# Two-layer MoE stack: the second experts' weights loaded from the inputs in five transfers per tile, and the fills of the recurrence issued in sixteen paced pieces

## The reference

```python
h = _layernorm(x) * (1 + ca) + sa
x = x + ga * _L0_attn_ref(h, ...)      # RWKV-6: 2 heads of 64, a recurrence over 1024 tokens
h = _layernorm(x) * (1 + cb) + sb
x = x + gb * _L0_ffn_ref(h, ...)       # top 1 of 16 experts, 128 -> 256 -> 128, gelu
h = _layernorm(x) * (1 + ca) + sa      # from here the second layer's modulation
x = x + ga * _L1_attn_ref(h, ...)      # 16 heads of 32, second-order linear attention
h = _layernorm(x) * (1 + cb) + sb
x = x + gb * _L1_ffn_ref(h, ...)       # the second experts
```

```python
h = silu(xf @ w1) * (xf @ w3)          # w1, w3: (expert, 128, 704)
y = h @ w2                             # w2: (expert, 704, 128)
out = sum of the two chosen y, weighted
```

## Time and profile before

| | us |
|---|---|
| median of 3 runs | 745.98 (743.45 to 750.7) |
| the profiled execution | 753.16 |
| its span | 751.4 |
| TensorE matmul busy | 676.9 (90%) |
| TensorE weight load busy | 571.8 (76%) |
| VectorE, ScalarE, GpSimd busy | 424.1, 303.3, 275.9 |
| share of the span at full TensorE clock, mean | 0.926 |
| SP's queue, transfers on 16 engines | 57.21 MB, 25.0% |
| instruction queues | 1.43 and 0.25 MB, 0.8% and 0.1% |

### The profile page before, as it was taken

The page is one execution under the profiler, slowest core; times in us unless marked ns, Lnnn a source line. Parts: engine busy times, 40 slices in busy tenths (PEclk is TensorE's granted clock), DMA queues, the critical chain, the costliest instruction groups (busy, mean ns, idle before and its releaser), DMA issues.

```text
span 751.4 us, 26349 instructions
## 1 busy us (share of the span) xinstructions
PE 676.9 (90%) x10932; PEld 571.8 (76%) x10932; DVE 424.1 (56%) x1342; ACT 303.3 (40%) x1017; POOL 275.9 (37%) x419
## 2 busy tenths in 40 slices
PE   5788989989756997999999999999999799999996
PEld 4466767668746985888878787888877698898995
DVE  3776786875421323567667666566766455444443
ACT  1455565542022413545544444444443243333321
POOL 2455564556462012024252425252423242222215
PEclk9699898896765997999999999899999899999999
DMA  7999000000055410000000000000040256657562
GB/s 198 311 335 193 2 2 2 3 8 23 22 166 153 135 46 9 3 10 6 16 18 11 18 10 18 10 15 15 11 146 12 85 208 212 220 202 239 180 218 62
DMA packets 50998, 66.73 MB, mean 89 GB/s; under 512 B 5424, under 2 KB 40464, under 8 KB 47936
## 3 DMA queue, kind: packets, MB, share of 16 engines
q1 hardware_dynamic: 44992, 57.21, 25.0%
q0 software_dynamic: 3424, 7.08, 2.9%
q10 hardware_dynamic: 2464, 0.76, 0.4%
HBM read 49.44 MB, written 19.91 MB: 92 GB/s over the span
## 4 chain that ended last, share of the span: by engine, by line
PE 53%; DVE 3%; DMA 2%; issue 2%; POOL 1%; another core or an unknown queue 1%; ACT 0%; SPq 0%; DVEq 0%; POOLq 0%
PE quad L1763 6%; PE bank L1905 5%; PE bank L1788 4%; PE quad L1887 4%; PE quad L1889 4%; PE pair L1725 3%; PE bank L1812 3%; DMA f_xg<-moe_slots 2%; PE bank L1825 2%; PE quad L1769 2%; PE pair L1727 2%; PE pair L1726 2%; PE bank L1828 2%; PE bank L1815 2%; PE pair L1750 2%; PE bank L1794 2%
## 5 line engine op out<-in xcount | busy, mean ns | idle before, releaser
L2162 DVE TENSOR_TENSOR h_masked<-quad,const 128x1536 f32<-128x1536 f32 (+2 forms) x66 | 112.5, 1704 | 67.6 <-PE quad L1769 45.4
L1999 ACT ACTIVATE f_sa<-quad 128x256 f32<-128x256 f32 (+1 forms) x115 | 40.2, 352 | 94.0 <-PE quad L1889 76.7
L2276 DVE TENSOR_TENSOR f_hid<-f_sa,quad 128x256 f32<-128x256 f32 (+1 forms) x115 | 43.0, 380 | 54.1 <-ACT f_sa L1999 53.9
L1887 PE MATMUL quad<-f_xT,wall 128*128 128x256 f32 (+1 forms) x190 | 51.3, 352 | 3.7 <-DVE f_hid L2276 3.6
L1905 PE MATMUL bank<-wall,f_hid 128*128 128x128 f32 x390 | 50.7, 277 | 1.1 <-DVE f_hid L2279 0.9
L1905 PEld LDWEIGHTS bank<-wall,f_hid 128*128 128x128 f32 x390 | 47.8, 192 | 3.6 <-DVE f_hid L2279 2.8
L1889 PE MATMUL quad<-f_xT,wall 128*128 128x256 f32 (+1 forms) x190 | 50.2, 346 | 0.0
L2385 POOL DMA_INDIRECT moe_slots<-g_pay,g_slot x28 | 28.4, 1013 | 59.2 <-DVE g_pay L2130 41.2
L1976 ACT ACTIVATE h_gT<-bank 128x128 f32<-128x128 f32 x64 | 17.8, 278 | 75.0 <-PE bank L1815 75.0
L1763 PE MATMUL quad<-h_qk 32*128 32x128 f32 x1024 | 48.0, 303 | 0.0
L1788 PE MATMUL bank<-h_qk,h_state 32*32 32x128 f32 x1024 | 45.8, 276 | 1.3 <-issue 1.2
(11 more groups left out here) (410 smaller groups left out, 1888.7 us busy)
## 6 DMA issues: line engine op xcount, KB each, us to landing
wall<-moe_w SPq DMA_DIRECT2D x23, 1088.0 KB, 5.2
moe_slots<-blank SPq DMA_DIRECT2D x2, 2112.0 KB, 25.6
wall<-in_experts_dram SPq DMA_DIRECT2D x1, 4120.0 KB, 21.6
e_w<-in_experts_dram SPq DMA_DIRECT2D x15, 257.5 KB, 3.0
moe_slots<-blank SPq DMA_DIRECT2D x1, 1984.0 KB, 9.6
moe_slots<-e_yg SPq DMA_DIRECT2D x7, 256.0 KB, 2.3
f_xg<-moe_slots SPq DMA_DIRECT2D x12, 132.0 KB, 4.3
moe_w<-in_moe_w_dram SPq DMA_DIRECT2D x1, 1408.0 KB, 7.6
```

Source lines behind the costliest of these rows:

```text
L1887: pe.matmul(up_bank(n, f)[:, 0:s], w[:, F1 + TAIL1 + f * P:F1 + TAIL1 + (f + 1) * P], x_of(n)[:, 0:s], start=True, stop=True)
L1999: act.activation(sa[g % 3][:, 0:s], up_bank(n, f)[:, 0:s], ACT.Silu).then_inc(f_sa, 1)
L2162: dve.tensor_tensor(masked[k % 4][:, :, a * P:z * P], quad[:, :, a * P:z * P], cst("causal")[:, None, a * P:z * P].to_broadcast([P, HPG, ( ...
L2276: dve.tensor_tensor(hid[n % 2][:, f, 0:s], sa[g % 3][:, 0:s], up_bank(n, f)[:, T1:T1 + s], ALU.mult)\
```

## The change

It has three parts. (1) The buffer `moe1_w`, its staging copies and its semaphore `s_w2` go away. `weights(n)` loads a tile's weights straight from the inputs `moe_w3`, `moe_w1` and `moe_w2` in five transfers, which all add to the tile's semaphore (80 in place of 16). (2) The zero rows of the last block of `w2` are written by three memsets of VectorE at the start of `layer1_phase`, once for each buffer, since the fifth transfer writes only the upper 64 partitions. (3) The three remaining fills are cut into 4, 4 and 8 pieces, and SP waits before each: piece n (0 to 15) is issued when `s_tot` has reached 2n + 1.

```diff
+SPARES, WALLS = ((0, 8), (8, 16), (16, 24), (24, 31)), 4
...
+FILLS1 = 8
+SLAB1 = SLOTS1 // T1 // (FILLS1 // 2)
...
             sp.wait_ge(s_set, 3)
-            staged = t["moe1_w"].rearrange("e p n -> p e n")
-            w1, w3 = t["moe_w1"].rearrange("e p n -> p e n"), t["moe_w3"].rearrange("e p n -> p e n")
-            sp.dma_start(staged[:, :, 0:F1], w3).then_inc(s_w2, 16)
-            sp.dma_start(staged[:, :, F1:F1 + TAIL1], w1[:, :, MAIN1:F1]).then_inc(s_w2, 16)
-            sp.dma_start(staged[:, :, F1 + TAIL1:2 * F1], w1[:, :, 0:MAIN1]).then_inc(s_w2, 16)
...
-            sp.dma_start(wall[:, :, :], t["experts0"].rearrange("e p n -> p e n")).then_inc(s_wall, 16)
+            def pace(n):
+
+                sp.wait_ge(s_tot, 2 * n + 1)
+
+            spare = t["moe0_slots"][0:USED_ROWS, :].rearrange("(q p) n -> p q n", p=P)
+            for n, (a, b) in enumerate(SPARES):
+                pace(n)
+                sp.dma_start(spare[:, a:b, :], blank[:, 0:1, 0:C].to_broadcast([P, b - a, C])).then_inc(s_slab, 16)
+            for n in range(WALLS):
+                e = slice(n * E0 // WALLS, (n + 1) * E0 // WALLS)
+                pace(len(SPARES) + n)
+                sp.dma_start(wall[:, e, :], t["experts0"][e].rearrange("e p n -> p e n")).then_inc(s_wall, 16)
             slots = t["moe1_slots"].rearrange("(q k p) n -> k p q n", k=2, p=P)
-            for k in range(2):
-                sp.dma_start(slots[k], blank[:, k:k + 1, :].to_broadcast([P, SLOTS1 // T1, PAY])).then_inc(s_fill, 16)
+            for n in range(FILLS1):
+                k, q = n % 2, slice(n // 2 * SLAB1, (n // 2 + 1) * SLAB1)
+                pace(len(SPARES) + WALLS + n)
+                sp.dma_start(slots[k][:, q, :], blank[:, k:k + 1, :].to_broadcast([P, SLAB1, PAY])).then_inc(s_fill, 16)
...
-                    pe.wait_ge(f_w[n % NB], n // NB * 16 + 16)
+                    pe.wait_ge(f_w[n % NB], n // NB * 80 + 80)
...
+            for k in range(NB):
+                dve.memset(wt[k][TAIL1:P, 2 * F1 + MAIN1:], 0.0).then_inc(f_blank, 1)
...
-            sp.wait_ge(s_w2, 16 * (5 + E1_LIVE))
             sp.wait_ge(s_early, 2)
...
-                sp.dma_start(wt[n % NB][:, :], t["moe1_w"][bass.ds(e, 1), :, :].rearrange("e p n -> p (e n)"))\
-                    .then_inc(f_w[n % NB], 16)
+                w, done = wt[n % NB], f_w[n % NB]
+                w2 = t["moe_w2"][bass.ds(e, 1), :, :]
+                sp.dma_start(w[:, 0:F1], t["moe_w3"][bass.ds(e, 1), :, :].rearrange("e p n -> p (e n)")).then_inc(done, 16)
+                w1 = t["moe_w1"][bass.ds(e, 1), :, :].rearrange("e p n -> p (e n)")
+                sp.dma_start(w[:, F1:F1 + TAIL1], w1[:, MAIN1:F1]).then_inc(done, 16)
+                sp.dma_start(w[:, F1 + TAIL1:2 * F1], w1[:, 0:MAIN1]).then_inc(done, 16)
+                sp.dma_start(w[:, 2 * F1:2 * F1 + MAIN1].rearrange("p (f n) -> p f n", f=FULL1),
+                             w2[:, 0:MAIN1, :].rearrange("e (f p) n -> p (e f) n", p=P)).then_inc(done, 16)
+                sp.dma_start(w[0:TAIL1, 2 * F1 + MAIN1:], w2[:, MAIN1:F1, :].rearrange("e p n -> p (e n)"))\
+                    .then_inc(done, 16)
```

More of the change, by code:

```diff
@@ L189, in bass_adaln_stack @@
                 layer1_phase(nc, t, const, x_sb, x_bc, eps_pow, sbw[:, 1], mod_col, mod_row, quad, bank, pair, cst,
-                             hT_all, W1, s_w1, s_w2, s_fill, gate_rows, yt, weight, slot0, s_back, wall, h_all,
+                             hT_all, W1, s_w1, s_fill, gate_rows, yt, weight, slot0, s_back, wall, h_all,
                              out)
@@ L1442, in up @@
                 if n == 0:
-                    pe.wait_ge(s_wall, 16)
+                    pe.wait_ge(s_wall, 16 * WALLS)
                 if n >= E0:
@@ L1898, in down @@
                 if n == 0:
-                    pe.wait_ge(f_blank, 2)
+                    pe.wait_ge(f_blank, 2 + NB)
                 for k in range(halves(n)):
```

21 lines of the change are left out of this document (5 added, 16 removed).

## The result

The changed kernel takes **760.4 us** (median of 4 runs, 755.94 to 762.93), the kernel before 746.8 (4 runs, 743.45 to 750.7): ratio 1.0151, 95% interval 1.0107 to 1.0195. The profiled execution of the changed kernel took 761.02 us, its span 759.2, against 753.16 and 751.4 before, so the profiled pair differs by 7.8 us only: the profiled execution of before was 6.3 us above its median, that of the changed kernel 0.6. All ratios here leave out executions that took over 1.5% longer than the fastest of their kernel; medians and mean clocks are over all.

A forecast was written before the change was run, and what follows sets the result against it. The recurrence was taken as a round trip through four engines, none full, and the tile loop as bound by TensorE's matmuls. -1.0 + 0.4 + 2.9 + 0 = +2.3 us on the median 745.98 gave 748.3 us, range 740 to 758.

The forecast's parts named there:

- The front: Start of the recurrence: staging removed and fills paced were to give -1.0 us, bounds -4.9 and +3.7.
- pacing halves the pressure: Recurrence: paced fills would come in bursts of some 8 to 9 us during the scans, leaving the DMA engines empty between.
- the stall of step 2: Recurrence, scan's small products: TensorE idle 2.27 us; with its clock worth 3.7 us, gone in somewhat over half of cases.
- the clean steps 1 and 3: Recurrence: the two steps read at 17.9 us each, one beside full DMA rings and one beside none.
- a step beside full rings is as fast as one beside none: Recurrence: bulk traffic as such does not slow the engines, so removing the staging is worth nothing directly.
- The memsets: Start of layer 1: three memsets on VectorE stand on the chain without cover, +0.4 us, bounds +0.3 and +0.5.
- The loop: Tile loop: five transfers delay the gather at seven odd tiles, +2.9 us, bounds -1.9 and 12.0.
- the gather lands 0.7 us later: Tile loop: later issue is covered, only shorter rows count, +0.5 for w2 and +0.2 for 256-byte rows.
- The end: After the last tile: the later gathers of the results were to cost 0, their 0.7 us delay being hidden.
- the other case: End of the kernel: if the whole 2.0 us of later issue counted, about 1.0 us would show.
- The cover of 1 us: End of the kernel: GpSimd's store lands at 746.9, VectorE's at about 748, so 1 us of delay is hidden.
- The second rival: Tile loop and end: each transfer costs its own time, 12.0 us in the loop and 1.0 at the end, 758.4; chance 0.15.

The follow-up runs named there:

- e1: The changed kernel measured again, against the kernel before on the same chip: 758.77 us against 751.60, ratio 1.0101.
- e15: e2 again on another chip: kernel before with only the fills in sixteen paced pieces, 720.25 us against 711.65, ratio 1.0070.
- e16: e15 without the waits, the same sixteen pieces issued one after the other: 712.48 us against 711.65 for the kernel before, ratio 0.9996.
- e2: Kernel before with only the fills in sixteen paced pieces, staging copies and one weight transfer per tile kept: 761.63 us against 751.60, ratio 1.0116.
- e4: Changed kernel with the three fills in one go, only the pacing undone: 763.37 us against 751.60 for the kernel before, ratio 1.0185.
- e17: e4 again on another chip (changed kernel, fills unpaced): 722.60 us against 712.44 for the kernel before, ratio 1.0154.
- e12: Kernel before with the staging copies issued a second time into an unread buffer: 750.69 us against 746.73, ratio 1.0064.
- e3: Kernel before with only the five transfers from the inputs and three memsets, staging copies made but unread: 756.91 us against 751.60, ratio 1.0118.
- e13: e3 again on another chip (five transfers from the inputs, staging unread): 722.05 us against 711.65 for the kernel before, ratio 1.0124.
- e9: Kernel before with a tile's weights loaded from the staging buffer in five transfers, w2 in long rows: 749.86 us against 746.73, ratio 1.0038.
- e10: Kernel before with three weight transfers, w3 and w1 together from staging, w2 in two from inputs, plus memsets: 748.00 us against 746.73, ratio 1.0024.
- e7: Kernel before with idle products added to TensorE in each step of the recurrence: 764.29 us against 753.39, ratio 1.0156.
- e6: Kernel before with four 64-byte HBM-to-HBM transfers between each tile's weights and its gather: 819.16 us against 753.39, no ratio given.

## Why the prediction was wrong

The kernel became 13.6 us slower (1.5%), and 7.2 us in e1, where I had forecast 2.3; 760.4 is above the forecast of 748.3 and above the range, which ended at 758. Point by point:

- **The front, -1.0 forecast.** This is the step that failed most: 5.1 us in the profiled pair. I had written that "pacing halves the pressure" and that the stall of step 2 would go in somewhat more than half of the cases. It did go. But I read the clean steps 1 and 3 as the kernel's normal state and the low clock as the consequence of a stall. The runs show that no such stall is needed: with idle times of 0.6 us at most the recurrence can fall into steps of 20.5 us, each with its own 7 us at half clock, and how often it does depends on when the traffic comes (e15 against e16). Pacing makes it fall in more often: mean clock 0.918 against 0.933 (e2) and 0.939 against 0.952 (e15), which cost 1.2% and 0.7% with one transfer per tile. In the changed kernel's profiled pair it was +4.1, beyond my upper bound of +3.7, and the medians carry more. Removing the staging copies, which I held to be worth nothing or a gain, may lower the clock too (e4, e17). And "a step beside full rings is as fast as one beside none" holds only where it has no stall: beside traffic there are steps of 18.6 to 19.0 us at clock 1.00 with a stall of 0.9 to 1.4 us in them (e12, e15, e17).
- **The memsets, +0.4.** Right: 0.42 us in the chain.
- **The loop, +2.9, bounds -1.9 to 12.0.** Right mechanism (all seven waits stand at the odd tiles 5 to 17, as forecast), mis-sized term: "the gather lands 0.7 us later". From the first weight issue to the gather's landing it was 1.62 + 4.2 = 5.8 us in the median, and now is 3.3 + 3.6 = 6.9, so 1.1. With that in my own sum it is 3 x 1.1 + 4 x (1.1 - 0.5) = 5.7, against 5.2 in the pair and 5.0 over all executions. As forecast, the landing time fell, and by less (0.6 us) than the issue moved (1.7): the gather does wait for bytes, but only in part. Between the two cases, nothing of the later issue shows and all of it does, I had put the landing too near the first.
- **The end, 0.** Wrong: +1.9. I had the price for the other case (1.0 of 2.0 shows) and chose the one of the loop, 0.7, though the last gather is issued 2.0 us later behind five transfers. The cover of 1 us that I had counted is not there either. VectorE's store did land at 748.1 as I had worked out, but the program then waited for GpSimd's DRAIN until 749.9, so a later first sum shows in full: `turn` 18 to the first sum took 28.8 to 29.1 us in every kernel with one transfer and 30.2 to 33.0 with five.
- **The second rival, "each transfer costs its own time" (758.4, chance 0.15), was nearest.** Its condition (the gather lands more than 2.7 us after its later issue) came true, 3.6. Its loop term of 12.0 did not: it was 5.2. Its total is close by luck, because the front's loss stands in for the rest.
- **The rule of the Trainium skill** on joining small transfers ("DMA: Bandwidth & Descriptors", "Rules for kernel authors") spoke against the change and the trace agrees: 3.4 of the loop's 5.0 us go with the number of transfers alone. I had set its weight too low.
- **What I said the profile would show.** The wait for `f_xg` at 5 us: it was 6.3. The gather's time to landing down by more than 1 us: it was 0.5 to 0.6. Bursts with DMA share about 1 for some 8 us: yes in steps 1 and 2 (1.04 and 1.02 from 54 to 60 us in step 1), shorter in step 3. Steps that all run at 17.9 did not come, and steps that all run at 20.5 were not on my list in either column.
- **The method.** I based the front on five steps of one execution. The clock of the kernel before ranges from 0.911 to 0.944 over 13 executions on one chip (b), and the time falls by some 5.5 us for each 0.01 (straight line through them). A single profile can't price such a thing, and neither end of my range had it.

Several things stay open. Alone, five transfers cost 1.2% (e3, e13) and pacing 1.2 and 0.7% (e2, e15), and both with the staging gone 1.0 to 1.5% (e1, the result): the parts do not add up. What the stall of the earlier trace rows and its eight fellows waited for is not shown, though their timing points at the loading of code. Most of all it is open why a recurrence with full rings over steps 1 and 2 stays out of the pattern. The Trainium skill, "TensorE: Matmul & The Clock Gate", section "Part 1: The HAM clock gate", says that the chip's activity window runs freely, so the same kernel meets it at different phases. By that rule a small shift of a step's start would decide, and beside full rings it is shifted, by 0.2 to 0.3 us in step 1 of e9 and e10 (18.2), though by nothing in e16 (17.9). The trace agrees that the same kernel shows both patterns, but no run here moved the phase alone.

## What to carry to other kernels

A transfer split into five on the queue that also carries the next stage's gather is paid at the gather: count the time from the release of the first issue to the landing of the last, at every place where that queue is followed, the last tile's too. Before counting on cover at the end, look for the instruction that ends the program; it need not be the last store. Before pricing a change near a stage whose clock is not steadily at full speed, look at several executions; a stage that repeats may have two lengths, and an edit that leaves its work alone can change how often each comes. The prepared layout that lets one transfer do a tile's work was worth 1.2% here (e3, e13), although its copies looked like waste.

## What the hardware showed that I had not expected

- Two lengths of the same step, each repeated for several steps, 17.9 and 20.5 us, with no difference in work or waits but 7 us at clock 0.50 in the latter, and 20.5 also where added products had cut that stretch to 3 or 4 us (e7).
- Four transfers of 64 bytes into HBM between a tile's weights and its gather cost 66 us over 19 tiles and 4 more, with landings of the gathers lengthened from 4 to 8 us (e6).
- GpSimd's DRAIN at the end of the block took 8.1 to 8.3 us in every profiled execution, some 6 us beyond its last sum, and ended the program after the last store had landed.
- Chips differ: the kernel before took 751.6, 753.4 and 746.7 us on three and 711.7 and 712.4 on two others. The loop is equal there (e15: 93.3, e16: 94.0). The two are faster ahead of it: layer 1's update of `h_state` runs from 287.4 to 515.6 us in e16 and from 305.7 to 553.3 before, 19.4 us shorter, and the layer starts 18 us earlier (memsets at 260.9 against 279.0). Between 300 and 420 us single products of the first kind take the same mean time in both (296 ns, line 1763 and its like), at granted clocks of 1.00 in e16 and 0.98 before over that update. The clock does not make the difference: in e9, on chip c and at 1.00, the update runs for 243.8 us, against 228.2 in e16. The cause is open.
